# Forming the last tile's product with x on TensorE while four tiles are left, with one unread stream fewer

## The reference, cut to what matters

```python
deg = jnp.sum(A, axis=0) + jnp.sum(A, axis=1) - jnp.diagonal(A)
d_inv_sqrt = jnp.where(deg > 0, jax.lax.rsqrt(deg), 0.0)
L_norm = d_inv_sqrt[:, None] * (jnp.diag(deg) - A) * d_inv_sqrt[None, :]
_, U = jnp.linalg.eigh(L_norm)
agg = jnp.einsum('mn,bnd->bmd', U.T, features)
h = jax.nn.relu(agg @ W1 + b1)
return jnp.einsum('nm,bmd->bnd', U, h @ W2 + b2)
```

## Time and profile before

| what | value |
|---|---|
| median of three runs | 5209.18 us |
| the profiled execution's own time | 5206.49 us |
| its span, first to last instruction | 5204.4 us |
| VectorE busy | 4276.0 us, 82% of the span |
| TensorE busy (matmuls) | 2719.4 us, 52% |
| ScalarE, GpSimd busy | 988.1 us, 945.6 us |
| mean granted TensorE clock | 0.718 of full |

### The profile page before, as it was taken

One profiled execution on the slowest core, in us unless ns is written; L12 is line 12 of the kernel. 1 busy time (PEld: TensorE's weight loads), 2 busy tenths in 40 slices (PEclk: granted clock), 3 DMA queues, 4 the chain that ended last, 5 costly groups with the idle time before them and its releaser, 6 DMA issues.

```text
span 5204.4 us, 67592 instructions
## 1 busy us (share of the span) xinstructions
PE 2719.4 (52%) x13544; PEld 2084.5 (40%) x13545; DVE 4276.0 (82%) x24022; ACT 988.1 (19%) x4375; POOL 945.6 (18%) x4428
## 2 busy tenths in 40 slices
PE   7999999999999888876661000000000010200476
PEld 6676777777767666666661000000000000100343
DVE  7979999988888788877778888887888889799424
ACT  2323333333333333322221000000000000000010
POOL 3422222222222233333331111111000000000000
PEclk9979999999998899975555555555555555655688
DMA  1000000000000000000000000000000000000001
GB/s 45 1 1 1 1 1 1 1 1 1 1 1 1 1 1 1 1 1 1 1 1 28 0 0 0 0 0 0 0 0 0 0 0 0 0 0 0 0 0 32
DMA packets 16093, 17.35 MB, mean 3 GB/s; under 512 B 3056, under 2 KB 12400, under 8 KB 15472
## 3 DMA queue, kind: packets, MB, share of 16 engines
q1 hardware_dynamic: 15216, 13.47, 0.8%
q10 hardware_dynamic: 512, 0.02, 0.0%
HBM read 9.25 MB, written 4.19 MB: 3 GB/s over the span
## 4 chain that ended last, share of the span: by engine, by line
DVE 58%; PE 29%; issue 7%; POOL 3%; ACT 2%; DVEq 1%; SPq 0%; DMA 0%; POOLq 0%; another core or an unknown queue 0%
DVE h L2122 6%; PE ps L737 5%; PE ps L698 4%; PE ps L791 3%; PE ps L724 2%; PE ps L668 2%; DVE am L1362 2%; DVE ps L1449 2%; DVE small L1463 2%; PE ps L654 2%; PE ps L716 2%; PE ps L676 1%; DVE hT L1749 1%; DVE junk L1436 1%; DVE eye L1436 1%
## 5 line engine op out<-in xcount | busy, mean ns | idle before, releaser
L698 PE MATMUL ps<-ident 128*128 128x256 f32 x2992 | 810.5, 410 | 0.0
L698 PEld LDWEIGHTS ps<-ident 128*128 128x128 f32 x2992 | 559.9, 200 | 66.7 <-issue 6.4
L737 PEld LDWEIGHTS ps<-UR 128*128 128x128 f32 x2552 | 378.2, 211 | 191.5 <-DVE UR L1520 93.8
L870 PE MATMUL ps<-ident,m 128*128 128x128 f32 x36 | 9.0, 429 | 823.0 <-DVE small L2222 823.0
L737 PE MATMUL ps<-UR 128*128 128x41 f32 (+17 forms) x2552 | 389.1, 284 | 92.5 <-ACT UR L1222 69.6
L814 PE MATMUL ps<-ones,qs 32*1 32x1 f32 x16 | 1.5, 158 | 821.4 <-DVE qs L1857 821.4
L1017 POOL TENSOR_SCALAR small<-small 128x1 f32<-128x1 f32 x511 | 118.3, 232 | 1224.3 <-ACT small L1186 1206.2
L870 PEld LDWEIGHTS ps<-ident,m 128*128 128x128 f32 x36 | 7.0, 223 | 825.0 <-DVE small L2222 825.0
L814 PEld LDWEIGHTS ps<-ones,qs 32*1 32x1 f32 x16 | 0.7, 76 | 822.4 <-issue 822.4
L2122 DVE RECIPROCAL h<-h 128x512 f32<-128x512 f32 (+2 forms) x50 | 295.6, 5913 | 1.7
L716 PE MATMUL ps<-UR,ident 128*128 128x18 f32 (+2 forms) x1020 | 232.5, 310 | 89.9 <-DVE UR L1451 89.9
(11 more groups left out here) (695 smaller groups left out, 8745.1 us busy)
## 6 DMA issues: line engine op xcount, KB each, us to landing
out<-xs SPq DMA_DIRECT2D x4, 1024.0 KB, 4.5
m<-in_adj SPq DMA_DIRECT2D x1, 1024.0 KB, 5.3
before<-c_before SPq DMA_DIRECT2D x1, 1024.0 KB, 6.1
notafter<-c_notafter SPq DMA_DIRECT2D x1, 1024.0 KB, 7.8
sib<-c_sib SPq DMA_DIRECT2D x1, 448.0 KB, 8.7
eye<-c_eye SPq DMA_DIRECT2D x1, 256.0 KB, 2.8
iota<-c_iota SPq DMA_DIRECT2D x1, 256.0 KB, 3.1
leafsel<-c_leaf SPq DMA_DIRECT2D x1, 256.0 KB, 3.2
```

The source lines that it names most:

```text
L698: nc.tensor.matmul(ps[1][:, 0:2 * P].rearrange("p (a d) -> p a d", a=2), ident[:, 0:P], ident[:, 0:P].unsqueeze(1).broadcast_to([P, 2, P]) ...
L737: last = nc.tensor.matmul(ps[2][:, 0:2 * npend + 3], over(x_of(j)), flat[:, j, 2 * first:2 * k + 3], start=(j == tp), stop=(j == T - 1))
```

## The change

Both edits are in two constants. `BY_TENSOR` goes from 5 to 4, so `product_by_tensor(k)` holds for the 127 steps with four tiles on (and for those with one, as before). In each of them VectorE has three instructions at `L1436` in place of four; TensorE has four more matmuls of one column, with the last tile's columns of each row tile as weights; ScalarE has one more copy of a column. And the streams of a four-tile step go from (2, 3, 5) to (2, 2, 4). Counted over k = 8 to 126: 77 steps go from five to four, 35 from three to two, and 7 (index 0) keep two.

```diff
-STREAMS = {4: (2, 3, 5), 3: (2, 2, 4), 2: (0, 0, 1), 1: (0, 0, 0)}
-BY_TENSOR = 5
+STREAMS = {4: (2, 2, 4), 3: (2, 2, 4), 2: (0, 0, 1), 1: (0, 0, 0)}
+BY_TENSOR = 4
```

## The result

The changed kernel takes 5257.97 us (median of 4 runs, 5248.97 to 5263.67) against 5208.69 us for the kernel before beside it: a ratio of 1.009, with a 95% interval of 1.0074 to 1.0106. It is slower by 49 us; the forecast was slower by 21 us. The direction held, and so did the mechanism (the clock falls); how far it fell did not.

The account below looks back on a forecast made before the run. VectorE was taken to come last, by little, in ordinary full-clock steps and TensorE at half clock. Full-clock gain -15, longer half-clock steps +11 and lower clock +25 gave +21 us: 5230 us, range 5190 to 5264.

Parts of the forecast that it names:

- Full-clock terms: Four-tile steps at full clock: VectorE's gain against TensorE's longer queue, -15 us in sum, bounds -30 and +5.
- the panel steps with an addition: 24 full-clock panel steps of index 3 to 6: VectorE's gain counts, -0.45 us each, -10.8 in all.
- those of index 0 to 2: 19 full-clock panel steps with some TensorE time to spare: -0.15 us each, -3 in all.
- Ordinary steps: Some 57 full-clock four-tile steps outside the panel steps: +0.05 us each, +3 in all.
- The +11 for longer half-clock steps: Half-clock four-tile steps, where TensorE is last: +0.94 us a step over 12 steps, +11 us.
- the price of 0.34: Four-tile stage: each us more at half clock costs 0.34 us of time.
- the clock's term: Four-tile stage: one-column passes replacing streams lower the clock, 74 us more at half clock, costing +25 us.
- I take 0.94 for it, 53 us more at half clock, and 21 us more for the part before 440 us: Four-tile stage: clock from 440 to 885 us falls from 1.00 to 0.94; 74 us more at half clock altogether.
- A: Rival on the four-tile stage: the clock stays as it is, -15 + 11 = -4 us, 5205 us; chance 0.22.
- B: Rival: TensorE's idle time before `L791` vanishes, and half-clock spells with it; 5157, or 5181 with half gone; chance 0.15.
- C: Rival: ScalarE's copy of the product is late and `L1476` waits, +36 us, 5241 us; chance 0.05.
- D: Rival: the four-tile clock falls much further, 160 us more at half clock, +54 us, 5259 us; chance 0.10.

Follow-up runs that it names:

- e3: Changed kernel with 128 columns in each pass of the product (x read with stride 0) in place of one: 5176.1 us, 0.9942 of the kernel before.
- e6: Changed kernel without the change in steps of index 0 to 5 (product on VectorE, three panel streams there): 5214.7 us, 1.0004 of the kernel before.
- e9: Kernel before with only the third stream of the 35 panel steps of index 1 to 5 removed: 5237.5 us, 1.0058 of the kernel before.
- e10: Kernel before with only the product moved to TensorE in the 42 steps of index 0 to 5: 5241.7 us, 1.0067 of the kernel before.
- e7: Kernel before with both halves of the change in steps of index 0 to 5 only: 5276.9 us, 1.0123 of the kernel before.
- e2: Changed kernel with the product back on VectorE, so only the streams are reduced: 5247.6 us, 1.009 of the kernel before.
- e1: Changed kernel with the streams back at (2, 3, 5), so only the product is on TensorE: 5266.7 us, 1.0115 of the kernel before.
- e11: Changed kernel with 128 columns a product pass and streams (2, 3, 3): 5175.6 us, 0.992 of the kernel before.

## Why the prediction was right in direction and wrong in size

- *Full-clock terms: -15, or -17 for all steps; measured about -21.* The product's queue time (0.88 predicted, 0.89 measured), the ordinary step bound by TensorE (6.3 to 6.45, measured 6.34), the panel steps with an addition (-0.45, measured -0.40) and those of index 0 to 2 (-0.15, measured -0.20) held. Ordinary steps came to -0.06 each where I took +0.05: the late ones lost as foreseen (6.04 to 6.34 at k = 121), but light Euler units gained more.
- *Half-clock price and the old spells.* The +11 for longer half-clock steps and the price of 0.34 were meant to cover 103 + 74 = 177 us, at a cost over before of 36 us. Measured: 257 us for 110, 0.43 a us, and 31 for 103 before, 0.30 a us. Per us that was added, the sum had 36 / 74 = 0.49 and 79 / 154 = 0.51 was measured, so the price of the two terms together came out nearly right. That is partly luck: the row behind the 0.34 was misread. The step of 8.59 us wasn't at half clock throughout but for 2 x (1 - 0.60) x 8.59 = 6.9 us of it:

```profile
419.54:428.13 8.59, 8.28 (x33) 6.97 (x32) 6.72 (x36) 2.73 (x11) 1.71 (x10) 0.60 0.00 0
```

  With it the price would have been (1.56 + 1.27) / 6.9 = 0.41, and the clock's term 30 us instead of 25.
- *"I take 0.94 for it, 53 us more at half clock, and 21 us more for the part before 440 us"*: this is the step that failed. Measured: 0.91 from 440 to 885 us, 80 us more; and 29 to 440 us went from 0.88 (the line below) to 0.79, which is 2 x 0.09 x 411 = 74 us more, not 21. In sum 154 us and not 74, with most of the miss before 440 us. The two terms together, 36 us, came to 110 - 31 = 79.

```profile
29.00:440.00 411.00, 375.33 (x1899) 291.12 (x1897) 349.71 (x1913) 123.51 (x556) 130.85 (x535) 0.88 0.00 1
```

- *Why it failed.* I compared stream passes per us over long stretches, 1.32, 1.17 and 0.91. The mean says little. In before, the seven panel steps from 485 to 532 us have 44 passes, 0.94 per us, next to the 0.91 of the bad stretch, and run at 1.00. The other columns count too: e3 shows it with `L698` unchanged. And the panel steps of index 1 to 5, which had three streams, lost a third of them, the ordinary ones a fifth. A comparison step by step would have shown that. I also spread the loss over 66 steps, of which the ordinary ones lost little in the changed kernel and, by the total of e6, nothing.
- *Rivals.* A (clock unchanged) and B (a busier TensorE keeps the clock) fell: 912 of 919 us busy, and a mean clock of 0.86. The rule of the Trainium skill ("TensorE: Matmul & The Clock Gate", section "Why this matters for your kernels") that throughput doesn't drop in mid-kernel where TensorE has no long idle gaps between its bursts would have had B. These runs disagree with it: in the changed four-tile stage TensorE waits for VectorE's `L1484` six times, 1.9 us at the longest, and no other wait of its is over 0.3 us (waiter, releaser, us in total, times, longest):

```profile
PE ps L791 <- DVE am L1484: 5.0, 6, 1.9
```

  C: the wait is 3.1 us in all. D (160 us more at half clock, 5259) is what happened, by the amount of the clock as by the time.

Two things stay open. e9 and e10 cost 24 and 28 us, e7 62, and their intervals reach some 15 to 20 us to each side, so whether the two halves simply add up in the panel steps or make each other worse isn't told. And whether `L784`'s passes, which use 32 of 128 rows, count less for the clock was not tried.

## What to carry to other kernels

Here 35 streams taken from the panel steps, which had three, cost 24 us (e9), and 77 more taken from the others, which had five, brought that to 42 (e2). So work out a change of such filler work step by step, not by the mean of a stage. When a product moves to TensorE as passes of one column, its passes take their 0.11 us anyway. Try reading the column with stride 0 up to 128 times: here nearly the same time (0.98 us for eight passes, not 0.89) kept the clock up, and some 80 us lay between one column and 128. And ask of every matmul that replaces a stream not how long it keeps TensorE busy but how many columns it moves.

## What the runs showed of the hardware that was not expected

- A TensorE busy 99% of the time (912 of 919 us) ran at 1.2 GHz for 28% of it. The eight passes of 128 columns took 0.98 us and those of one column 0.89.
- The unchanged two-tile stage differs from execution to execution: the clock was 0.91 in before (633 us long), 0.83 in e1 (666 us), 0.87 in e10 and, in the slowest of e11's eleven runs, 5215.5 us against a median of 5175.6, as low as this:

```profile
1598.00:2271.00 673.00, 608.20 (x2808) 471.95 (x2807) 530.59 (x3828) 246.09 (x1169) 189.61 (x1017) 0.81 0.00 1
```

  That is 673 - 633 = 40 us in a stage whose code is the same, as much as this execution lies above the median of its kernel. What tips it was not found, nor whether a change in the four-tile stage has a part in it.
